# Attention stage: values of two tiles at a time, three score banks, and four ones sums moved into the next head

## What is computed

```python
qkv = x @ attn_qkvw + attn_qkvb
q, k, v = ...                       # (1, 32 heads, 2048, 32)
scores = jnp.einsum('bhqd,bhkd->bhqk', q, k) * scale
probs = jax.nn.softmax(scores, axis=-1)
ctx = jnp.einsum('bhqk,bhkd->bhqd', probs, v)
```

## Time and profile before

| | us |
|---|---|
| median of 3 runs | 2847.87 |
| lowest, highest | 2843.93, 2850.26 |
| the profiled execution | 2850.67 |
| its span, first to last instruction | 2848.9 |
| TensorE busy in the span | 2751.8 |
| POOL busy | 1733.5 |
| VectorE busy | 1637.0 |
| ScalarE busy | 1289.9 |
| mean granted clock of TensorE, share of full | 0.978 |

### The profile page before, as it was taken

The page is one execution under the profiler, slowest core; times in us unless marked ns, Lnnn a source line. Parts: engine busy times, 40 slices in busy tenths (PEclk is TensorE's granted clock), DMA queues, the critical chain, the costliest instruction groups (busy, mean ns, idle before and its releaser), DMA issues. The chain is left out here.

```text
span 2848.9 us, 36121 instructions
## 1 busy us (share of the span) xinstructions
PE 2751.8 (97%) x13776; PEld 1612.5 (57%) x13776; DVE 1637.0 (57%) x2553; ACT 1289.9 (45%) x2299; POOL 1733.5 (61%) x406
## 2 busy tenths in 40 slices
PE   7999999999799999999999999999999999997999
PEld 6888887778444444444444444444444444436887
DVE  8411111111778777777777778777877787724221
ACT  3111111110066666666666666666666666672100
POOL 0111111110199989898999899889989998982121
PEclk9999999999599999999999999999999999998999
DMA  4233333112611121112111211221122111004432
GB/s 140 98 129 112 110 110 111 66 66 89 162 27 38 38 60 34 38 38 60 35 41 35 60 35 42 45 50 38 38 51 44 38 38 35 9 16 144 128 103 92
DMA packets 145852, 188.56 MB, mean 66 GB/s; under 512 B 87152, under 2 KB 112240, under 8 KB 134896
## 3 DMA queue, kind: packets, MB, share of 16 engines
q1 hardware_dynamic: 145712, 186.70, 23.6%
HBM read 122.44 MB, written 63.69 MB: 65 GB/s over the span
## 5 line engine op out<-in xcount | busy, mean ns | idle before, releaser
L859 DVE TENSOR_REDUCE part_max<-ps_b 128x1 f32<-128x512 f32 x2048 | 1276.2, 682 | 399.8 <-PE ps_b L740 398.0
L706 POOL TENSOR_TENSOR psum_p<-psum_p,probs 128x2048 f32<-128x2048 f32 x316 | 1455.9, 4607 | 47.1 <-ACT probs L837 1.4
L837 ACT ACTIVATE probs<-ps_b 128x512 f32<-128x512 f32 x2048 | 1114.1, 597 | 743.7 <-PE ps_b L730 742.2
L730 PE MATMUL ps_b<-qp,kp 97*128 97x512 f32 x2048 | 880.4, 434 | 1.4 <-ACT probs L837 1.3
L740 PE MATMUL ps_b<-kp,qp 96*128 96x512 f32 x2048 | 765.7, 417 | 50.2 <-DVE part_max L859 35.6
L730 PEld LDWEIGHTS ps_b<-qp,kp 97*128 97x128 f32 x2048 | 386.3, 189 | 627.3 <-ACT probs L837 453.8
L758 PE MATMUL ps_b<-probs,vh 128*32 128x512 f32 x4096 | 556.5, 616 | 2.5
L740 PEld LDWEIGHTS ps_b<-kp,qp 96*128 96x128 f32 x2048 | 400.4, 196 | 146.7 <-DVE part_max L859 80.6
L232 POOL TENSOR_TENSOR wlo<-wraw,whi 128x1024 fp32r<-128x1024 f32 x29 | 69.5, 2397 | 612.7 <-ACT whi L335 612.7
L261 PE MATMUL ps_a<-xhi,whi 128*128 128x512 f32 (+1 forms) x928 | 370.7, 399 | 1.0 <-DVE elo L424 0.9
L261 PE MATMUL ps_a<-xlo,whi 128*128 128x512 f32 (+1 forms) x928 | 367.7, 396 | 0.0
(11 more groups left out here) (72 smaller groups left out, 1100.5 us busy)
## 6 DMA issues: line engine op xcount, KB each, us to landing
kp<-qk_scr SPq DMA_DIRECT2D x96, 256.0 KB, 4.1
qp<-qk_scr SPq DMA_DIRECT2D x96, 256.0 KB, 6.3
qk_scr<-ehi SPq DMA_DIRECT2D x16, 1024.0 KB, 3.9
qk_scr<-elo SPq DMA_DIRECT2D x16, 1024.0 KB, 6.7
wraw<-wcat SPq DMA_DIRECT2D x29, 512.5 KB, 7.5
craw<-cz_scr SPq DMA_DIRECT2D x16, 768.0 KB, 5.0
stage<-x SPq DMA_DIRECT2D x16, 512.0 KB, 4.4
v_scr<-elo SPq DMA_DIRECT2D x16, 512.0 KB, 3.3
```

What stands on the lines that cost most here:

```text
L706: pool.tensor_tensor(acc[:, :], (acc if n else probs[0])[:, :], probs[t % RING][:, :], ALU.add) \
L730: pe.matmul(ps[:, st_bank(g, j, b), :], kp[j][0:PACK + 1, t * P:(t + 1) * P], qp[j][0:PACK + 1, b * NQ:(b + 1) * NQ], start=True, stop=Tru ...
L837: act.activation(probs[t % RING][:, b * NQ:(b + 1) * NQ], ps[:, st_bank(g, j, b), :], ACT.Exp, scale=SCALE).then_inc(exp_done, 1)
L859: dve.tensor_reduce(part_max[jn % 2][:, tn, b:b + 1], ps[:, MAX_BANK + bank, :], AX_X, ALU.max) \
```

## The change

- `LEAD` is 4. The transposition stays after step 13 (the last of the next head's maxima are now made in step 11, and were in step 12).
- `values` run for two tiles at a time, after the eight score matmuls of every even step: tiles `t - 2` and `t - 1` in steps 2 to 14, tiles 14 and 15 in step 0 of the next head. In the last head they run for one tile in each step.
- The scores for the exponentials rotate through three PSUM banks everywhere, the last head included (two, and four in the last head, before). The other five: one for the context, four in a ring that the maxima, the transposition and the sums share. The sums of a head hold one of them from step 0 to step 4 of the next head; in between the maxima have three.
- POOL adds tiles 0 to 11. Tiles 12 to 15 stay in a ring of ten `probs` buffers; TensorE sums 12 and 13 in step 0 and 14 and 15 in step 2 of the next head, and POOL's total in step 4.
- The normalisation is for the head before last and in four instructions of 128 columns, behind the second maximum of steps 1 to 4. The reciprocal comes after step 7.
- Keys, queries and values have three slots; SP loads for two heads ahead, stores the context of the head before last ahead of the spread of sums.

```diff
-POOL_TILES = [0, 1, 2, 3, 4, 6, 7, 8, 9, 11, 12, 14]
+POOL_TILES = [0, 1, 2, 3, 4, 5, 6, 7, 8, 9, 10, 11]
+LATE_SUMS = {0: [12, 13], 2: [14, 15]}
 LAST_POOL_TILES = [0, 1, 2, 3, 4, 6, 8, 10]
...
-LEAD = 3
-POOL_SUMS_AT, TAKE_SUMS_AT, RECIPROCAL_AT, NORMALISE_AT = 3, 4, 8, 10
-RING = 8
-SLOTS = 4
+SLOTS = 3
+RING = 10
+LEAD = 4
+TRANSPOSED_AT = TT - LEAD + 1
+SUMS_AT, RECIPROCAL_AT, NORMALISE_AT = 4, 7, 1
...
-        ST_BANKS, MAX_BANKS = 2, 4
-        MAX_BANK, PV_BANK, SUM_BANK = 2, 6, 7
+        ST_BANKS, RING_BANKS = 3, 4
+        RING_BANK, PV_BANK = 3, 7
...
+        ring_order = []
+        for h in range(-1, HEADS):
+            for t in range(first_step(h), TT):
+                if has_maxima(h, t):
+                    ring_order += [("max", h, t, b) for b in range(QB)]
+                if t == 0 and h >= 1:
+                    ring_order.append(("sum", h - 1, 0, 0))
+                if t == SUMS_AT and h >= 1:
+                    ring_order.append(("given back", h - 1, 0, 0))
+                if t == TRANSPOSED_AT and h < LAST:
+                    ring_order.append(("flip", h + 1, 0, 0))
...
+            def step(h, t):
+                for b in range(QB):
+                    if h >= 0:
+                        scores_t(h, t, b)
+                    if has_maxima(h, t):
+                        scores(h, t, b)
+                if h < 0:
                     return
...
+                if t == 0 and h >= 1:
+                    values(h - 1, TT - 2)
+                    values(h - 1, TT - 1)
+                if h < LAST:
+                    if t % 2 == 0 and t >= 2:
+                        values(h, t - 2)
+                        values(h, t - 1)
+                elif t >= 1:
+                    values(h, t - 1)
+                    if t - 1 in LAST_ONES_TILES:
+                        late_sum(h, t - 1)
+                if h >= 1:
+                    for tl in LATE_SUMS.get(t, []):
+                        late_sum(h - 1, tl)
+                    if t == SUMS_AT:
+                        pool_sum(h - 1)
...
+            def normalise(h, part):
+                c = slice(part * P, (part + 1) * P)
...
+                dve.tensor_tensor(out_ctx[h % 2][:, c], raw_ctx[h % 3][:, c], recip_b[:, c], ALU.mult) \
                     .then_inc(ctx_ready, 1)
...
+                    for b in range(QB):
+                        if has_maxima(h, t):
+                            take_max(h, t, b)
+                        if b == 1 and h >= 2 and 0 <= t - NORMALISE_AT < QB:
+                            normalise(h - 2, t - NORMALISE_AT)
+                    if t == RECIPROCAL_AT and h >= 1:
+                        reciprocal(h - 1)
```

More of the change, by code:

```diff
@@ L585, in target @@
[L585 to L618, removed]
+        def target(h, t):
+            return (h + 1, t + LEAD) if t + LEAD < TT else (h + 2, t + LEAD - TT)
@@ new lines, in pool_adds, with pool_count, late_tiles, slot @@
+        def pool_adds(h):
+            return (len(POOL_TILES) - 1) * h
+        def pool_count(h, t):
+            return pool_adds(h) + max(1, pool_tiles(h).index(t))
+        def late_tiles(h):
+            return LAST_ONES_TILES if h == LAST else sum(LATE_SUMS.values(), [])
+        def slot(h, t):
+            return (TT * h + t) % RING
+        def tile(h, t):
+            return probs[slot(h, t)]
+        previous = {}
+        held = {}
+        for h in range(HEADS):
+            for t in range(TT):
+                previous[h, t] = held.get(slot(h, t))
+                held[slot(h, t)] = (h, t)
@@ L695, in _, with add @@
             pool.wait_ge(ones_done, SLOTS + 1)
[L697 to L715, removed]
+            def add(h, t):
+                n = pool_tiles(h).index(t)
+                acc = psum_p[h % 2]
+                if n == 1:
+                    wait(pool, sum_ready, h - 1)
+                else:
+                    pool.wait_ge(pool_done, pool_adds(h) + n - 1)
+                pool.wait_ge(exp_done, 64 * h + 4 * t + 4)
+                first = acc if n > 1 else tile(h, pool_tiles(h)[0])
+                pool.tensor_tensor(acc[:, :], first[:, :], tile(h, t)[:, :], ALU.add).then_inc(pool_done, 1)
+            for h in range(HEADS):
+                for t in pool_tiles(h)[1:]:
+                    add(h, t)
         @block.tensor
@@ L720, in _ @@
             pe.wait_ge(ones_done, 1 + SLOTS)
[L722 to L737, removed]
-                if tn == 0 and b == 0:
[L739 to L748, removed]
@@ L756, in values @@
                     wait(pe, raw_done, h)
                 for b in range(QB):
[L758 to L765, removed]
-                    return
-                if t == mine[0]:
-                    wait(pe, sums_taken, number(g, j))
-                for b in range(QB):
-                    last = pe.matmul(ps[b * HD:(b + 1) * HD, SUM_BANK, :], ones[:, :],
-                                     probs[t % RING][:, b * NQ:(b + 1) * NQ], start=(t == mine[0]), stop=False)
-                last.then_inc(pv_done, 1)
@@ L807, in _, with sum_of @@
-            scheduled(pe, period)
-            values(*LAST, TT - 1)
-            sums(*LAST, TT - 1)
-            pool_sums(*LAST)
+                    last = pe.matmul(ps[b * HD:(b + 1) * HD, PV_BANK, :], vh[h % SLOTS][:, t, :],
+                                     tile(h, t)[:, b * NQ:(b + 1) * NQ], start=(t == 0), stop=(t == TT - 1))
+                last.then_inc(pv_done, 1)
+            def sum_of(bank, data, start, stop):
+                for b in range(QB):
+                    last = pe.matmul(ps[b * HD:(b + 1) * HD, bank, :], ones[:, :], data[:, b * NQ:(b + 1) * NQ],
+                                     start=start, stop=stop)
+                return last
@@ L918, in project_output @@
+                    if t == TRANSPOSED_AT and h < LAST:
+                        take_transposed(h + 1)
+            for part in range(QB):
+                normalise(LAST - 1, part)
+            dve.wait_ge(sum_ready, HEADS)
+            dve.wait_ge(ctx_ready, QB * LAST)
+            dve.reciprocal(recip_b[:, :], ps[:, ring_bank[("sum", LAST, 0, 0)], :]).then_inc(recip_done, 1)
+            for part in range(QB):
+                normalise(LAST, part)
 def project_output(nc, x, w2, bias, cz_scr, w_early, early_loaded, out):
```

320 lines of the change are left out of this document (166 added, 154 removed).

## The result

The changed kernel takes 2824.2 us (median of 4 runs, 2818.9 to 2829.7) against 2847.3: ratio 0.9919, 95% interval 0.9895 to 0.9943, so 0.5 to 1.1% faster. The forecast was 2811, range 2762 to 2860: right in direction and range, 23 us gained where 36 were forecast. The profiled execution has a span of 2824.9 us, against 2848.9.

A forecast was written before the change was run, and what follows sets the result against it. TensorE, busy 543 of 556 us, was taken as the bound, POOL's 52.0 us a head as floor. Terms -41 - 6.5 + 2.4 + 6 + 2 + 0.5 = -36.6 from 2850.7 gave 2814, 2811 for the median; range 2762 to 2860.

The forecast's parts named there:

- price of a block beyond its tiles: TensorE going from scores to values and back: 0.37 us a block, eight blocks fewer a head save 3.0 us.
- quarter three: Third normalisation quarter on VectorE, due at 9.73, waits for POOL's sum until 11.82; the eighth M goes 2.34 us later.
- 0.2 by which the same sum missed: Remainder added to a head: the same sum gave 55.4 us for the old head against 55.66 in the trace.
- clock, mean of a head: Lower TensorE clock behind a stall: 0.8 us a head, half of bounds 0 to 1.55.
- heads 0 and 1: Heads without an earlier head's normalisation: 2.9 and 3.6 us saved, the second stopping at POOL's 52.0; 6.5 together.
- four more maxima ahead: Ahead of head 0, bound by VectorE: 4 x 0.59, +2.4 us.
- last head: Three T banks for four: the fourth T waits for the first exponential, 1.08 instead of 0.71 us, 16 times, +6.0.
- pairs without M (head 30): Eight T follow without M at head 30's end: ScalarE adds 1.4 us twice, less 0.8 of old waits, +2.
- (a): Rival: smaller stalls, port shared by bandwidth (0.92 us a quarter, 2774 us) or clock stays up (2788 us); chance 0.23.
- (b): Rival: POOL's floor, quarters slip into POOL's gaps; head 52.1 us, time 2730 us; chance 0.07.
- (c): Rival: slower, stalls in steps 2 and 4 bring the clock down in every head; 57.2 us, time 2878; chance 0.12.
- (d): Rival: pairs save nothing since V behind V pays the switch again; head 57.9 us, time 2895; chance 0.06.

The follow-up runs named there:

- before_one_input: The kernel before with its 512-column normalisation as a copy with one SBUF input, division left out: 2785.4 us, ratio 0.9771.
- whole_at_quarter3: The changed kernel with the normalisation as one 512-column instruction behind the second maximum of step 3: 2856.6 us, ratio 1.0014 to the kernel before.
- short_pool_one_input: The changed kernel with each quarter a one-input copy, division left out, and tiles 10 and 11 in no sum: 2732.4 us, ratio 0.9609.
- single_one_input: The changed kernel with each quarter a one-input copy, division left out, and values for one tile after every step: 2766.5 us, ratio 0.9704.
- one_input: The changed kernel with each quarter of the normalisation a VectorE copy with one SBUF input, division left out: 2733.2 us, ratio 0.9586.
- phased_two_banks: The changed kernel with quarters three and four behind the first maximum of steps 4 and 5, two banks for exponentials' scores, five in the ring: 3063.1 us.
- whole_step1: The changed kernel with the normalisation as one 512-column instruction behind the second maximum of step 1: 2743.5 us, ratio 0.9623.
- quarter3_later: The changed kernel with quarter three two maxima later, behind the fourth maximum of step 3: 2789.3 us, ratio 0.9806.

## Why the forecast was right, and where it was off

Step by step, by the profiled executions (24.0 us less in the span; from the first M to TensorE's last sum of POOL's total 1833.0 and 1808.3):

| step | forecast | measured |
|---|---|---|
| price of a block beyond its tiles | 0.37 us | 0.33 |
| stall around step 2 | 0.5 | 0.5 |
| quarter three | 2.1 | 2.10 |
| M behind it late by | 2.3 in all | 2.05 + about 0.25 behind it |
| "0.2 by which the same sum missed" | 0.2 | 0.26, behind the transposition |
| ScalarE's copy of the sums | 0.2 | 0 |
| head without a fall of the clock | 54.1 | 54.0 |
| clock, mean of a head | 0.8 | 1.3 |
| 29 heads | -41 | -28.4 |
| heads 0 and 1 | -6.5 | -6.4 |
| four more maxima ahead | +2.4 | 0 |
| last head | +6 | +10.1 |
| pairs without M (head 30) | +2 | in the 29 heads |
| four quarters at the end | +0.5 | +0.2 |

**The pairs.** Right in mechanism, 2.6 us in place of 3.0. The entry into a block is 0.32 us behind an M here, where 0.36 stood in the step I took it from, in which a T came last. The same kernel with singles and three banks has heads of 53.2 against 54.1 in `before_one_input`, so 0.9 of what I counted as the old step belongs to its two-bank order; the runs do not separate bank count from order. What makes a switch cost 0.33 us, no run shows. In the time of a head the pairs gave 1.1 us and not 2.6, for the three banks took part of it back.

**The quarters.** The schedule laid out by hand held nearly to the tenth: quarters of 0.28, 2.97, 2.10 and 2.30 us, two and four in the shadow of blocks, three in the open. The terms as measured close: 50.9 for TensorE's blocks and scores, 0.5 around step 2, 2.3 in step 4 and 0.26 behind the transposition are 54.0. One reading was off: the stall of 1.57 us that I took for the old kernel is that of three heads in 29; the others have 1.25 to 1.4. The same sum then misses the old head by 0.5 and not by 0.2, so that 54.1 against 54.0 is in part luck. That the end of POOL's running sum decides is shown by three runs: one input, another place, another size at the same place.

**The clock** is the term that was mis-sized: "I take half, 0.8". The rows for the stall of 1.41 us and its 12 heads of 30 were a poor base for one of 1.88, the more so as most of those stalls were shorter than the one laid out. In the changed kernel 20 of 29 heads are long, six of them by two falls' worth: 55.32 - 53.98 = 1.3 us a head, 15 us over what I charged, more than the whole miss of 13. The forecast said that TensorE would idle longer here and still split the bounds in the middle; the mean lies inside the bounds, near their upper end. But the upper bound rests on one fall a head, and six heads have two: in `whole_at_quarter3` heads of one fall (55.7) and of two (57.0) alternate, at 1.3 a fall some 2 us a head, more than the bound allows.

**The last head** cost 10.1 us and not 6. Its fourth T comes 1.27 us behind the first (2505.30 and 2506.57) and not 1.08, since ScalarE starts 0.62 behind the first T there and not 0.43: 0.56 late in each step, 8.4 from the first sum on. The other 1.7 are two ones tiles of head 30, which now stand behind that sum and which I did not count.

**POOL** was no bound in any steady head, as forecast, with 2.8 to 4.3 us idle ahead of the first sums above. Its own price was 51.2 us and not 52.0. Heads 0 and 1 came out as forecast in their sum only: I gave the first to TensorE and 52.0 to the second, and POOL holds both at 51.2. With less work for POOL (`short_pool_one_input`) they take 48.4 and 51.8, so TensorE would have been 2.2 us quicker over the two. The four maxima ahead cost 2.6 us at the transposition (771.55 to 774.15) and were given back by the first sum (785.09 to 785.35), since no values stand between the first scores any more.

**The rivals.** (a) did not come: the quarters that met POOL mostly took 2.1 to 3.0 us where a share of bandwidth gives 0.92, one of 512 at the same place took 0.6 more and not four times as much, and the clock fell. (b), POOL's floor, did not come either, since quarter three was due 1.95 us ahead of an end. (c) did not come, but `whole_at_quarter3` shows its mechanism, with one stall of 2.65 us instead of two: 2857 us, no faster than before. (d), pairs that save nothing, is excluded by 33 us between `single_one_input` and `one_input`. Two sums were slightly off: by its own terms (d) gives 2899 and not 2895, and the forecast with the clock always falling 2833 and not 2837.

## What to carry to other kernels

Before an instruction with two SBUF inputs is put on VectorE beside a POOL that reads SBUF, look where POOL's instructions end: place it just ahead of an end, inside a block that covers it, or where POOL is idle. Cutting it into pieces multiplies the waits, for here each piece that met a running sum waited for its end. And price a stall of TensorE together with the lower clock that may follow it, from rows of stalls of the same length: the stall of 2.05 us had 1.3 us a head of lower clock behind it, that of 2.65 about 2.

## What the runs showed of the hardware

The Trainium skill (SBUF — State Buffer, "SBUF: two separate sides") describes an exclusive lock between a GpSimd instruction and a VectorE one with two SBUF inputs. The runs agree: 128 columns took 0.28 us alone and up to 4.67 with POOL at work (they ended 0.15 us behind its sum, 512 columns 0.55), 512 columns 0.68 and 2.70 at two places of the same kernel, and one input (with the other operation) made both 0.28 and 0.68 everywhere. Once, in `phased_two_banks`, it was POOL that was held up: four quarters that began 0.04 us behind the start of a sum took 0.27 us each, and that sum took 5.33 us instead of 4.58.

The clock against the longest stall of a head (distance of two score starts, less 0.235 us), by the granted clock of each head:

| longest stall, us | heads in which the clock fell |
|---|---|
| 0.6 (`whole_step1`), 0.9 (`quarter3_later`), heads 3 to 29 | none |
| 1.25 to 1.4 (before, heads 2 to 30) | 10 of 26 |
| 1.6 (before, heads 2 to 30) | 3 of 3 |
| 2.05 (after, heads 2 to 30; 3.2 in head 2) | 22 of 29, six for twice as long |
| 2.65 (`whole_at_quarter3`, heads 2 to 30; 4.9 in head 2) | all 29, 16 for twice as long |

A fall adds 1.3 to 1.6 us to most heads; in head 30 of the kernel before and in heads 2 and 30 of the changed one it does not show in the length. The longest stall isn't all of it. In head 30 of `one_input`, where eight T follow each other and wait for ScalarE again and again, none longer than 0.46 us, the clock fell too:

```profile
2390.00:2394.00 4.00, 4.00 (x21) 1.00 (x24) 0.00 (x0) 1.30 (x4) 3.92 (x2) 0.57 0.00 0
```

Behind quarter three of the changed kernel the granted clock is 0.63 on average in 3.8 us, part at 1.2 and part at 2.4 GHz:

```profile
1563.70:1567.50 3.80, 3.73 (x17) 1.38 (x21) 3.80 (x5) 1.19 (x2) 3.80 (x1) 0.63 0.02 4
```

After most waits of TensorE of over 0.1 us the next start comes 0.34 us later instead of 0.235 (1563.77 to 1564.11 in the changed kernel), so three waits of 0.2 us cost half as much again. POOL's sums follow each other by 4.65 us in the changed kernel and by 4.73 in the old one, with the same 4.58 of work; the order of its two waits was changed with them, and nothing here shows that this is the cause.
